# Mamba layers of a hybrid block: the convolution as four shifted projections, B and C rows through DRAM, C products on two engines, the scan's ring in x's buffer

## What is computed

```python
mu = jnp.mean(src, axis=-1, keepdims=True)
var = jnp.mean((src - mu) ** 2, axis=-1, keepdims=True)
s = (src - mu) * jax.lax.rsqrt(var + EPS) * ln_g + ln_b
x1, x2 = jnp.split(s, 2, axis=-1)
h = x1
for i in range(NL):                      # 2 layers, NS = 16 states, DI = 256 channels
    h = h + _mamba_block(_rmsnorm(h, rms_w[i]), in_W[i], conv_w[i], ...)
...
def _mamba_block(x, inW, cw, cb, xpW, dtW, dtb, A_log, Dp, moW):
    xc, z = jnp.split(x @ inW.T, 2, axis=-1)
    xc = silu(causal_depthwise_conv4(xc, cw) + cb)
    dt, Bm, Cm = split(xc @ xpW.T)       # 8 | 16 | 16
    delta = softplus(dt @ dtW.T + dtb)
    dA, dBx = exp(delta[..., None] * -exp(A_log)), (delta * xc)[..., None] * Bm
    # per channel and state: h = dA * h + dBx ; y = sum over states of h * C
    y = (y + Dp * xc) * silu(z)
    return y @ moW.T
```

## Time and profile before

| what | value |
|---|---|
| median of 3 runs | 3235.23 us (3234.01 to 3236.96) |
| profiled execution: span, first to last instruction | 3233.9 us |
| busy over the span | PE 2652.1, DVE 2058.3, ACT 2049.0, POOL 946.5 us |
| mean granted TensorE clock | 0.934 of 2.4 GHz |
| `mamba_layers`, first to last scan starts | 1939.7 to 3108.4 us |
| DMA traffic | 19.71 MB in all, mean 6 GB/s |

### The profile page before, as it was taken

One profiled execution on the slowest core, in us unless ns is written; L12 is line 12 of the kernel. 1 busy time (PEld: TensorE's weight loads), 2 busy tenths in 40 slices (PEclk: granted clock), 3 DMA queues, 4 the chain that ended last, 5 costly groups with the idle time before them and its releaser, 6 DMA issues. The chain is left out here.

```text
span 3233.9 us, 48264 instructions
## 1 busy us (share of the span) xinstructions
PE 2652.1 (82%) x16052; PEld 1125.7 (35%) x16052; DVE 2058.3 (64%) x3560; ACT 2049.0 (63%) x2908; POOL 946.5 (29%) x726
## 2 busy tenths in 40 slices
PE   4799999999999999959988776777777776766769
PEld 2333332222222222237777652222222222222237
DVE  6664332231311000079885749999999999999987
ACT  2477778888888888826554246666666655555623
POOL 0000000000000000001111226666666666566722
PEclk8899999999999999979999888889998898999989
DMA  2000000000000000000000000000000000000001
GB/s 118 1 1 1 1 1 0 1 1 0 1 0 0 0 0 0 0 14 15 13 14 1 1 1 0 0 1 1 0 0 1 0 0 1 1 0 0 0 0 52
DMA packets 4182, 19.71 MB, mean 6 GB/s; under 512 B 448, under 2 KB 448, under 8 KB 3520
## 3 DMA queue, kind: packets, MB, share of 16 engines
q1 hardware_dynamic: 4032, 17.90, 1.5%
HBM read 13.70 MB, written 4.19 MB: 6 GB/s over the span
## 5 line engine op out<-in xcount | busy, mean ns | idle before, releaser
L346 ACT ACTIVATE ga_probs<-ga_score 128x1024 f32<-128x1024 f32 x896 | 867.7, 1021 | 114.0 <-PE ga_score L402 107.2
L1870 POOL TENSOR_TENSOR mb_dbx<-mb_u,mb_bsb 128x1024 f32<-128x1024 f32 x256 | 607.8, 2386 | 353.2 <-ACT mb_bsb L1888 243.6
L402 PE MATMUL ga_score<-ga_qT,ga_kT 128*128 128x512 bf16 (+3 forms) x2304 | 620.3, 366 | 34.7 <-ACT ga_probs L346 3.0
L2258 DVE TENSOR_TENSOR_SCAN mb_hs<-mb_a,mb_carry,mb_dbx 128x512 f32<-128x512 f32 x512 | 627.9, 1269 | 5.4 <-POOL mb_dbx L1870 3.0
L1888 ACT ACTIVATE mb_a<-mb_delta,mb_decay_neg 128x512 f32<-128x512 f32 x512 | 349.9, 691 | 382.5 <-DVE mb_hs L2258 377.8
L2112 PE MATMUL mb_y<-mb_hc,identf 128*128 128x512 f32 x1024 | 541.0, 656 | 2.5 <-DVE hT L2218 2.2
L649 DVE TENSOR_TENSOR x<-x,ga_bank_b 128x256 f32<-128x256 f32 x32 | 13.5, 421 | 754.5 <-PE ga_bank_b L449 754.5
L402 PEld LDWEIGHTS ga_score<-ga_qT,ga_kT 128*128 (+1 forms) x2304 | 157.6, 98 | 601.1 <-issue 346.1
L2106 PE MATMUL mb_c<-mb_bc,mb_pick 96*128 96x512 bf16 x256 | 109.3, 427 | 293.7 <-DVE mb_hc L2226 293.7
L2226 DVE TENSOR_TENSOR mb_hc<-mb_hs,mb_c 128x1024 f32<-128x1024 f32 x256 | 307.3, 1200 | 3.3 <-issue 1.8
L2112 PEld LDWEIGHTS mb_y<-mb_hc,identf 128*128 128x128 f32 x1024 | 215.4, 212 | 169.9 <-issue 143.4
(11 more groups left out here) (333 smaller groups left out, 3772.9 us busy)
## 6 DMA issues: line engine op xcount, KB each, us to landing
x<-in_x SPq DMA_DIRECT2D x8, 512.0 KB, 8.9
la_xr<-in_x SPq DMA_DIRECT2D x8, 512.0 KB, 3.6
out_x<-x SPq DMA_DIRECT2D x8, 512.0 KB, 2.6
wd<-in_wd SPq DMA_DIRECT2D x1, 1793.0 KB, 19.9
wa<-in_wa SPq DMA_DIRECT2D x1, 1217.0 KB, 5.5
wb<-in_wb SPq DMA_DIRECT2D x1, 1153.0 KB, 13.8
wc<-in_wc SPq DMA_DIRECT2D x1, 1024.0 KB, 16.1
```

Of the source, the lines that this page charges most:

```text
L346: nc.scalar.activation(probs[:, j % 2, pr, :], score[pr][:, :], ACT.Exp, scale=SCORE_SCALE).then_inc(exp_done, 1)
L402: last = mm(dst, kcol, qT[:, c % 2, kv * GQ + 2 * pr + a, q0:CH], start=True, stop=j is None)
L1870: gp.tensor_tensor(dbx[:, n % RX, :, :], u[:, b, :, :], bsb[:, n % RB, :].unsqueeze(1).to_broadcast([P, 2, CH]), ALU.mult).then_inc(dbx_do ...
L2258: v.tensor_tensor_scan(hs[:, n % RH, half, :], abank[half][:, :], dbx[:, n % RX, half, :], carry[:, n, half:half + 1], ALU.mult, ALU.add). ...
```

## The change

In `mamba_norms`:

- SP loads `g.cw`, the conv weights spread over the partitions (1 MB), and stores x, chunk by chunk, to DRAM (`x_saved`); the stage's block ends when the last store has landed. GpSimd multiplies `g.cw` by the x half of the in-projection, one 1024-wide product per layer, which gives four weight matrices per layer.

In `mamba_layers`:

- In-projection of x and convolution become one sum of four matmuls per half (`in_x`), each tap with its own weights and with the input shifted by one token; the 3 tokens ahead of the chunk are copied in front of it (`move_tail`). Bias is added in the copy from PSUM, and Silu takes both halves in one instruction. VectorE's `convolve` is gone.
- B rows: the projection is saved to DRAM (64 KB) and loaded back broadcast to all partitions, four states at a time (1 MB) into two slots. `rows_b`, `copy_b` and the PSUM bank for B are gone.
- C products of states 0, 4, 8 and 12 are made on GpSimd, with C rows from DRAM as well (two loads of 512 KB per chunk), three steps later; `add_state` of these comes in step n+4. The other 12 stay on VectorE.
- The scan's output ring `hs` has 8 slots and lies in x's buffer. Carries are copied four states at a time. `mb_a` has three banks. `mo_proj` writes to `fbank[0]`.
- Relu of dt goes into `delta` itself.
- The loops over chunks are written out.

In `mamba_out` SP loads x back, chunk by chunk.

```diff
+        GRP, RB, RX, RH, RC, RP, RA = 4, 8, 4, 8, 3, 2, 3
+        hs = g.x[:, :, :].rearrange("p (s h q) d -> p s h (q d)", s=RH, h=2)
...
+            def in_x(f, half, t0, t1, out=fbank[1]):
+                l, _, b = place(f)
+                if t0 == 0 and half == 0:
                     pe.wait_ge(hn_ready, f + 1)
+                    pe.wait_ge(tail_moved, f + 1)
+                elif t0 == 0 and out is fbank[1]:
+                    pe.wait_ge(x_copied, f * 2 + 1)
+                for k in range(t0, t1):
+                    last = mm(out[:, :], g.cw[:, l, k, half * P:(half + 1) * P], hn[:, b, k:k + CH],
+                              start=(k == 0), stop=(k == TAPS - 1))
```

ScalarE's loop over the steps, the decay exponentials first and then the pieces:

```diff
                 for n in range(NS):
                     for half in range(2):
-                        s = 2 * n + half
-                        if before or s >= 2:
-                            act.wait_ge(scan_done, m * HS + (s - 1))
+                        s = m * HS + 2 * n + half
+                        if s >= RA:
+                            act.wait_ge(scan_done, s - RA + 1)
                         at = (l * 2 + half) * NS + n
...
                         if n == 6:
-                            project(f, fb, before)
-                        if n in (7, 9):
-                            abs_relu(f, fl, (n - 7) // 2)
+                            project(f)
+                        if n in (8, 9):
+                            abs_relu(f, n - 8)
+                        if n == 9:
+                            exp_e(f)
                         if n == 10:
-                            exp_e(f)
-                        if n == 11:
                             ln_e(f)
-                    if far:
...
-                        if n == 1:
-                            square(f, fl, fc)
-                        if n == 7:
+                    if m < LAST - 1:
+                        f = m + 2
+                        if n == 0:
+                            square(f)
+                        if n == 3:
                             rms(f)
-                        if n == 8:
-                            move_tail(f, fc)
-                        if n in (9, 11):
-                            copy_x(f, (n - 9) // 2)
+                        if n == 4:
+                            move_tail(f)
+                        if n in (8, 11):
+                            copy_x(f, (n - 8) // 3)
                         if n in (13, 15):
                             copy_z(f, (n - 13) // 2)
```

TensorE's loop after the change:

```diff
+                for n in range(NS):
+                    if n in DS:
+                        rows_c(m, n)
+                    if n == 0 and m:
+                        add_state(m - 1, NS - 1)
+                        add_state(m - 1, NS - 4)
+                    if n and n - 1 in DS:
+                        add_state(m, n - 1)
+                    if n - 4 in PS:
+                        add_state(m, n - 4)
+                    if m and n == 3:
+                        mo_proj(m - 1)
+                    if m < LAST:
+                        if n in (4, 5):
+                            x_proj(m + 1, n - 4)
+                        if n in (7, 8):
+                            dt_proj(m + 1, n - 7)
+                    if m < LAST - 1:
+                        f = m + 2
+                        if n == 2:
+                            mean_sq(f)
+                        if n in (6, 7):
+                            in_x(f, 0, 2 * (n - 6), 2 * (n - 6) + 2)
+                        if n in (9, 10):
+                            in_x(f, 1, 2 * (n - 9), 2 * (n - 9) + 2)
+                        if n in (12, 14):
+                            in_z(f, (n - 12) // 2)
```

SP's loop, which issues all DMAs of the stage:

```diff
+            for m in range(LAST + 1):
+                load_b(m, 2)
+                load_b(m, 3)
+                if m < LAST:
+                    save_rows(m + 1)
+                    load_c(m + 1, 0)
+                    load_b(m + 1, 0)
+                    load_b(m + 1, 1)
+                    load_c(m + 1, 1)
```

More of the change, by code:

```diff
@@ L29 @@
 NL, NS, DTR, TAPS = 2, 16, 8, 4
+POOL_STATES = (0, 4, 8, 12)
+DVE_STATES = tuple(n for n in range(NS) if n not in POOL_STATES)
 HALVES = 2
@@ L1778, in mamba_layers @@
         da_done, scan_done = sem("da_done"), sem("scan_done")
         y_read, yz_ready, mo_done, h_added = (sem(n) for n in ("y_read", "yz_ready", "mo_done", "h_added"))
-        HS = 2 * NS
         def slab(ap, c):
[L1783 to L1799, removed]
-                body(chunk(l, c, b), before, chunk(l, c + 1, 1 - b), chunk(l, c + 2, b))
-            first(chunk(0, 0, 0), chunk(0, 1, 1))
-            for l in range(NL):
-                for c in range(2):
-                    turn(l, c, c)
-                with eng.Fori(1, NCH // 2 - 1) as i:
-                    for b in range(2):
-                        turn(l, i * 2 + b, b)
-                for c in (NCH - 2, NCH - 1):
-                    turn(l, c, c % 2)
-            last(chunk(NL - 1, NCH - 1, 1))
@@ new lines, in _ @@
+            fn(decay[:, :], w("A_log"), ACT.Exp).then_inc(w_ready, 1)
+            act.wait_ge(consts, 5)
+            square(0)
+            rms(0)
+            move_tail(0)
+            for half in range(2):
+                copy_x(0, half, front[half])
+            for half in range(2):
+                copy_z(0, half, front[2 + half])
+            square(1)
+            silus(0)
+            project(0)
+            rms(1)
+            abs_relu(0, 0)
+            move_tail(1)
+            abs_relu(0, 1)
@@ L2009, in body @@
+            exp_e(0)
+            for half in range(2):
+                copy_x(1, half, front[half])
+            ln_e(0)
+            for half in range(2):
+                copy_z(1, half, front[2 + half])
+            act.wait_ge(decay_ready, 1)
+            act.wait_ge(x_copied, 4)
+            act.wait_ge(z_copied, 4)
+            for m in range(LAST + 1):
+                l, c, b = place(m)
                 act.wait_ge(delta_ready, m + 1)
@@ new lines, in in_z, with x_proj @@
+            def in_z(f, half, out=fbank[1]):
+                l, _, b = place(f)
+                if out is fbank[1]:
+                    pe.wait_ge(x_copied, f * 2 + 2)
+                    if half:
+                        pe.wait_ge(z_copied, f * 2 + 1)
+                mm(out[:, :], w("in_WT", l)[:, DI + half * P:DI + (half + 1) * P], hn[:, b, PAD:], start=True, stop=True).then_inc(z_done, 1)
+            def x_proj(f, half):
+                l, _, b = place(f)
+                if half == 0:
+                    pe.wait_ge(xc_ready, f + 1)
@@ L2111, in add_state @@
                 for half in range(2):
[L2112 removed]
+                    last = mm(ybank[half][:, :], g.identf[:, :], src[:, half, :], start=(n == order[0]), stop=(n == order[-1]))
                 last.then_inc(y_acc, 1)
[L2115 to L2132 removed]
@@ L2163, in last @@
-            def last(end):
-                m, l, c, b = end
-                add_state(m, NS - 1)
-                mo_proj(m, l)
-            turns(pe, first, body, last)
+            pe.wait_ge(consts, 5)
+            mean_sq(0)
+            for half in range(2):
+                in_x(0, half, 0, TAPS, front[half])
+            for half in range(2):
+                in_z(0, half, front[2 + half])
+            mean_sq(1)
+            for half in range(2):
+                x_proj(0, half)
+            dt_proj(0, 0)
@@ L2342, in turn @@
                     measure(c - 1)
-            pairs(dve, turn)
+            for c in range(NCH):
+                turn(c, c % 2, c >= 2)
             measure(NCH - 1)
```

552 lines of the change are left out of this document (267 added, 285 removed).

## The result

| | us, median of the runs | mean chunk, us |
|---|---|---|
| kernel before | 3236.1 (4 runs beside it) | 75.2 |
| changed kernel | 3361.4 (4 runs, 3360.9 to 3362.3) | 82.8 |

The changed kernel takes 1.0388 times as long, 95% interval 1.0374 to 1.0403. The forecast was 3259, so the sign was right and the size was five times too small: 125 us more instead of 24. The mean chunk is the distance from the third `mb_u` (the product u of a chunk, which VectorE makes once in each) to the fifteenth, divided by 12. Between the profiled executions (spans 3233.9 and 3359.1) the first `mb_u` comes 9.3 us later, the way from it to the second takes 8.1 more, the thirteen after that 100.0, the last 6.3, and the end 1.5.

What follows compares the result with a forecast made beforehand. VectorE was taken to bound the kernel. Per chunk, 57.0 us of work, 14.8 of waits and 4.6 of clock made 76.4 instead of 75.05; with the other chunks and ends +24, so 3259 us, range 3185 to 3300.

Steps and rivals of the forecast that it cites:

- VectorE's work: Mamba stage, per chunk: scans, 12 C products, closing y and small operations left on VectorE come to 57.0 us.
- the waits at full clock: Per chunk, VectorE's scans wait for ScalarE, queued behind TensorE results started one step before: 14.5 to 14.9 us together.
- S(9): Start of VectorE's scans of step 9: delayed by dt_proj's Abs and Relu and a copy of taps, wait 2.6 us.
- S(10): Start of step 10's scans: dt_proj behind taps and two sums, then Abs, Relu and exponential, wait 3.7 us.
- S(12): Start of step 12's scans: held by step 11's copy_x behind two taps, wait 1.2 us.
- S(14): Start of step 14's scans: held by step 13's copy_z behind two sums and in_z, wait 3.5 us.
- y: Step 1 of a chunk: y waits for two state sums on TensorE, not one, 1.4 us.
- Rival (b): TensorE's clock holds over idle stretches under about 5 us: chunk 71.8 us, 3194 us; chance 0.22, for two drops 0.12.
- the step on the clock: Three long TensorE idle stretches per chunk drop its clock, 1.6 us each less 0.2 of slack: 4.6 us.
- (d): Rival: TensorE stays at the low clock longer, chunk over 79 us, 3295 us; chance 0.06.
- my 1.35 each: 14 chunks that prepare one two ahead take 76.4 us each instead of 75.05: +19 us.
- Rival (c): ScalarE's waits are softer than read, VectorE bound at 57 to 60 us per chunk: 3016 us; chance 0.08.

Runs made afterwards that it cites:

- filled: Changed kernel plus matmuls of zeros in TensorE's idle stretches (steps 1, 9, 11, 13, 15): 3211.9 us, ratio 0.9926 to the kernel before.
- before_late: Kernel before with its TensorE pieces (mean square, dt_proj, in_proj) one step later, ScalarE's unmoved: 3375.8 us, ratio 1.0439 to the kernel before.
- pe_early: Changed kernel with its TensorE pieces (dt_proj, mean square, conv taps, z projection) one step earlier, ScalarE's unmoved: 3114.8 us, ratio 0.9625 to the kernel before.
- early_tuned: pe_early with dt_proj ahead of the state's sum, state 12 summed in step 15, GpSimd's split at step 9 instead of 8: 3110.2 us.
- tuned2: early_tuned with GpSimd's softplus at steps 13 and 14 and conv's second half wholly at step 9: 3081.3 us.
- tuned2_fill: tuned2 with matmuls of zeros in steps 1, 13 and 14: 3055.1 us, ratio 0.9440 to the kernel before.

## Why the prediction was right and wrong

**Right: VectorE's work.** 57.0 us per chunk; the sampled chunks have 81.7 - 24.2 = 57.5 and, filled, 72.5 - 15.1 = 57.4.

**Right: the waits at full clock,** place by place, against the filled kernel and the changed one (us):

| | S(9) | S(10) | S(12) | S(14) | S(0) | y | S(3) | S(4) | S(7) | sum |
|---|---|---|---|---|---|---|---|---|---|---|
| forecast, full clock | 2.6 | 3.7 | 1.2 | 3.5 | 0 | 1.4 | 0.7 | 0.9 | 0.5 | 14.5 |
| filled | 3.06 | 3.69 | 1.24 | 3.56 | 0 | 1.43 | 0.66 | 0.83 | 0.64 | 15.1 |
| changed kernel | 3.06 | 3.69 | 2.60 | 6.62 | 1.45 | 3.12 | 0.66 | 2.37 | 0.64 | 24.2 |

The chunk of 71.8 was measured as 72.5. Rival (b), the clock that holds, was priced at 3194; holding it by force gives 3212.

**Wrong: the step on the clock.** It had "three long ones per chunk", 1.6 us each, 4.6 in all. The trace has five, and they cost the 9.1 us between the table's last two rows; by the mean chunks it is 82.8 - 72.5 = 10.3. The 5.7 us between that and 4.6 are, 14 times, 80 of the 101 us that the forecast lacked. The three stretches that it counted came as said: 4.66, 4.72 and 5.96 us long for 4.9, 4.9 and 6.3, and they cost 1.36 at S(12), 1.45 at S(0) and 1.54 at S(4), together 4.35 for 4.6. What failed is the count: the stretch of 3.12 ahead of step 12's sums cost 3.06 at S(14), and the one of 2.91 ahead of the sum of state 15 cost 1.69 at y, and the forecast had both at nothing. Two errors are in it. First, I took one row, 3.61 us idle and nothing lost, to mean that stretches of 3 us are harmless. The changed kernel lost clock behind 3.12 and 2.91 us. The trace of before had rows that warned of it, in the same chunk on TensorE's timeline, and I bounded without them:

```profile
2296.36 0.61 PE L2106 MATMUL mb_c<-mb_bc,mb_pick 96*128 96x512 bf16 x1 [4.04 <-DVE mb_hc L2226]
2296.76 3.21 PE L2112 MATMUL mb_y<-mb_hc,identf 128*128 128x512 f32 x4
...
2322.90 3.39 PE L2095 MATMUL mb_y<-mb_yz,wd 128*128 128x512 f32 x4 [2.76 <-DVE mb_yz L2214]
```

Second, I put the upper bound of a stretch at 1.65 us, which is what one state's sum of 1.88 loses. At step 12 two sums and more stand ahead of what the scan waits for, both at the low clock (3.78 and 3.18 us), and the wait grew by 3.06. The bound should have been taken over all matmuls between the idle stretch and the waiter. Built so, with five stretches (four of 1.65 and one of 3.3), the upper bound of the term is 9.9, still 0.4 under what the mean chunks show, a chunk 81.7, and the time 14 x 6.65 = 93 us longer before the edges, near 3330. The rival nearest in number was (d), a low clock that stays longer, with 0.06; as a mechanism it fits step 12 alone. Its own sum is wrong besides: 76.4 + 2 x 1.65 is 79.7 us per chunk, which gives 3305 and not 3295, outside the stated range.

**Smaller:** the thirteen chunks between the second `mb_u` and the fifteenth cost 100.0 us, where my 1.35 each gives 18. The start came 9.3 late instead of 3: TensorE ends `mamba_norms` 1.3 later, its wait ahead of the first chunk is 6.19 us instead of 3.34, which is the 3 for the store of x, and 5.1 come behind it, where the front's conv taps run partly at the low clock (6.40 us for eight at 1907.26 on TensorE, 3.60 for the next eight); no run tries that part. The loads of rows were priced at 5 us per MB and no cost: 4.6, and none. Rival (c), softer waits of ScalarE, is in no trace: S(9) and S(10) waited 3.06 and 3.69 us at either clock, as forecast. The expected face of the profile was right in kind: VectorE at 70%, waiting for `mb_a`, clock 0.84, with five dips and not three.

**What stays open.** Why a stretch of 3.61 us left the clock alone and one of 2.91 did not; runs show only that filling the stretches removes the loss. In `before_late` two stretches of 2.08 and 2.14 us, with one short matmul between them, were followed by the low clock, so a stretch is not to be judged without its neighbours. How much of the 9.6 us of `before_late` is clock was not tried. How the 121 us of `pe_early` divide among its four moved pieces was not tried.

## What to carry to other kernels

When work leaves the bound engine, the next bound is often no engine but a ring: TensorE makes a piece, ScalarE reads it in order, and VectorE waits for what ScalarE queued behind the read. Count for each piece the steps between maker and reader, before and after; one step less cost 9.6 us per chunk here with no other change, the dips of the clock that it opened included, and one step more gained 17. Price the clock on the whole run of matmuls between an idle stretch and the one who waits, for every stretch near those that the trace shows to end at the low level; whether the price falls due is told by who waits there, since filling gave 150 us in the changed kernel, 13 in the kernel before, 2 in `pe_early`, 12 in `early_tuned` and 26 in `tuned2`.

## What the hardware showed that I had not expected

Useless matmuls that nobody reads made the changed kernel 4.5% faster (3361.4 to 3211.9), by taking the granted clock of the stretch from about 0.85 to 1.00. An idle stretch of 2.91 us was followed by a low clock and one of 3.61 in the kernel before was not, so the length of one stretch alone doesn't tell. And the exclusion of VectorE and GpSimd appears only as the rest gets tighter: `mb_u` takes 1.22 us in the changed kernel, 2.17 in `pe_early` and 2.48 in `tuned2_fill`, and `mb_w` 0.69, 0.69 and 1.71.
